# Attention on one core: the mixing of two neighbouring sets in one burst of ten rounds instead of two bursts of five

## Chip, cores, metric

One core of one Trainium2 chip. The time is device microseconds of the whole kernel on that core; lower is better.

## What is computed

The input x is (2, 8, 256, 512): two entries, eight channels, 256 rows (features) of 512 columns. The reference normalises it by groups, runs an attention layer with a residual, normalises again, and runs a 3x3 convolution on a sphere with a residual. The change touches only the attention core of the first layer:

```
qk = jnp.einsum('bceqd,bcekd->bceqk', q, k) / math.sqrt(h)
a = jax.nn.softmax(qk, axis=-1)
o = jnp.einsum('bceqk,bcekd->bceqd', a, v)
...
return _conv(_mcl(o, Wo, bo), o_conv_w, o_conv_b, 0)
```

For every entry and channel (16 in all) there are 8 heads of width 32 over 512 positions. `Wo` is a 256x256 product per channel that follows.

## The kernel before, in words

Three parts run one after the other: `front` (normalisation, projections, convolutions, rotary embedding, to about 410 us), `attend` (attention and the product with `Wo`, to about 979 us) and `blend` (the rest). The change is in `attend`.

One entry and channel is a **unit** (16 units), cut into 32 **steps**: a step is one head and one block of 128 rows or keys. For each step there are

- a row score matmul (L940, 128x512 into one of three PSUM tiles `a_row`) and on VectorE the maximum of each row (L1013). A row matmul waits until the maximum of three steps earlier is done (L938 and L939: `pe.wait_ge(max_done, step - ROWS + 1)`). These maxima serve the next unit.
- a column score matmul (L961, 128x512 into one of two PSUM tiles `a_col`) and on ScalarE its exponential (L1060) into `a_prob`. The column matmul waits for the exponential of two steps earlier (`exp_done, step - 1`).
- the low bf16 part of that exponential (`a_pl`): 26 of 32 steps on GpSimd (L1109), every fifth step on VectorE (L1024), in VectorE's queue right behind the row maximum of that slot.

Four steps are a **set** (eight sets g0 to g7 a unit). `mix_set` (L965 to L985) takes a set's `a_prob` and `a_pl` and does five **rounds**: two that sum the weights (L975) and three that mix the values (L984). A round is four matmuls of 512 columns into four 32-column strips of the array, which run side by side. `a_prob` and `a_pl` are rings of five sets; the first exponential of a set waits for `mixed` of five sets earlier.

After the fourth set of each half unit ScalarE takes the logarithm of the weights (L1065) and inverts it (L1072), and VectorE multiplies (`divide`, L1032, which waits for `inverted`). Once a unit there are four tail parts on TensorE (L998, the product with `Wo`, float32), two copies on ScalarE (L1078), the turning of the maxima (`turn_max` L950, `keep_max` L1048, `load_max` L1052), and the split of the values (`v_high` L1044 on ScalarE, `v_low` L1103 on GpSimd).

The order on each engine is written out by a small scheduler: `pipeline` has one slot for each step of the whole stage; every kind of work is given a slot, and an engine issues slot by slot, in a slot in the order in which the kinds are listed. On TensorE that is: turning, column score, row score, sets, tail parts. The row score of step t of unit n stands in slot 32n + t, the column score in 32n + 42 + t, mixing of set g in 32n + 54 + 4g, tail parts in 32n + 86, 88, 91 and 93, turning in 32n + 35, the half units' logarithm, inverse and `divide` in 32n + 67 and 83, `keep_out` (the copies) in 32n + 90 and 95, `v_high` in 32n + 40. `sets` (L857 and L858) gives the slots of the mixing and is used by TensorE's queue alone. VectorE's low parts stand in slots whose number modulo 32 is 3, 8, 15, 20, 25 and 30 (written as slots of one cycle of 32: 67, 72, 79, 84, 89 and 94).

```
pipeline(units(TURN, turn_max) + steps(EXP, col_scores) + steps(0, row_scores) + sets(MIX, mix_set) + tail_parts(TAIL, tail))
...
pipeline(steps(0, row_max) + units(SPLIT, split_max) + lows(EXP + 1, low_part, False) + quads(KEEP, divide))
```

Of the kernel before, what the change touches and what calls it, by code (L numbers as in the profile page):

```python
# [725 lines left out]
def attend(nc, T, QK, V, Z, mixing, q0, k0, qk0_in):  # L726
# [9 lines left out]
    with ExitStack() as ctx:  # L736
# [3 lines left out]
        STEPS = HEADS * QT  # L740
        UNITS = B * C
        PAIR = B * CHANNELS
        QUAD = P // DH
        SETS = HEADS // QUAD * QT
# [110 lines left out]
            return [(STEPS * n + first + t, lambda n=n, t=t: emit(n, t)) for n in range(UNITS) for t in range(STEPS) if low_on_pool(t) == on_pool]  # L855

        def sets(first, emit):  # L857
            return [(STEPS * n + first + QUAD * g, lambda n=n, g=g: emit(n, g)) for n in range(UNITS) for g in range(SETS)]  # L858

        def quads(first, emit):  # L860
            return [(STEPS * n + first + QUAD * QT * m, lambda n=n, m=m: emit(n, m)) for n in range(UNITS) for m in range(SETS // QT)]
# [70 lines left out]
        def _(pe):  # L932
# [55 lines left out]
            def tail(n, j, part):  # L988
# [10 lines left out]
                if part == PARTS - 1:  # L999
                    last.then_inc(out_full, 1)  # L1000

            pipeline(units(TURN, turn_max) + steps(EXP, col_scores) + steps(0, row_scores) + sets(MIX, mix_set) + tail_parts(TAIL, tail))

        @block.vector
# [669 lines left out]
```

## Time and profile before

| what | value |
|---|---|
| median of 3 runs | 1253.46 us (1249.54 to 1255.03) |
| the profiled execution's own time | 1252.62 us |
| its span | 1250.7 us |
| TensorE busy, whole span | 1075.9 us (86%) |
| VectorE busy | 922.9 us (74%) |
| ScalarE busy | 659.8 us (53%) |
| GpSimd busy | 871.0 us (70%) |
| first and last burst of mixing | 449.8 us and 970.6 us |

Engines in the profile: PE is TensorE (PEld its weight loads), DVE VectorE, ACT ScalarE, POOL GpSimd. Matmuls overlap: the profile gives a 512-column matmul about 0.4 us from start to end, while the next one starts about 0.22 us after it. What counts for TensorE's queue is therefore the distance between starts. In a timeline row the first number is the start, the second the length of what was merged into the row, and the bracket the idle time of the engine ahead of it with what ended it.

### The profile page before, as it was taken

The numbers are of one execution on the slowest core, as the hardware profiler recorded it, in microseconds if no ns is written. First come the engines' busy times: TensorE is split into PE (matmuls) and PEld (weight loads), VectorE is DVE, ScalarE is ACT, GpSimd is POOL, SyncE is SP. The second block draws the span as 40 slices with busy tenths as digits, with TensorE's granted clock in tenths as the row PEclk, the third lists the DMA queues.
The fourth block names the chain that finished last, engine by engine and source line by source line (L and its number), as shares of the span: only waits on it lengthen the run. The fifth ranks groups of instructions, "written<-read, shape, count | busy, mean of one in ns | idle before, by whom it ended". The sixth has DMA issues, their size and how long they took to land. (4 is left out here: it accounts for less than half of the span.)

```text
span 1250.7 us, 25719 instructions
## 1 busy us (share of the span) xinstructions
PE 1075.9 (86%) x10392; PEld 569.9 (46%) x10392; DVE 922.9 (74%) x1225; ACT 659.8 (53%) x1110; POOL 871.0 (70%) x812
## 2 busy tenths in 40 slices
PE   0299999999894699899999999999988599899998
PEld 0177777777673123333333333333333245455553
DVE  3789999999763798788888888888872585544344
ACT  1555555455442066566666676666666233346345
POOL 0467776777583499889998888988899006937900
PEclk9899999999997599999999999999998899899999
DMA  9725243332644545526171726254100599875661
GB/s 306 243 81 161 75 124 114 107 90 74 140 107 103 110 77 133 105 58 114 51 120 35 127 61 111 60 92 75 39 19 17 177 367 295 266 236 156 194 211 54
DMA packets 137757, 158.99 MB, mean 127 GB/s; under 512 B 17852, under 2 KB 85708, under 8 KB 137640
## 3 DMA queue, kind: packets, MB, share of 16 engines
q1 hardware_dynamic: 113448, 119.37, 39.8%
q10 hardware_dynamic: 15648, 28.81, 6.7%
q0 software_dynamic: 8544, 9.18, 2.8%
q8 instruction: 82, 1.34, 0.5%
q14 instruction: 35, 0.29, 0.1%
HBM read 106.48 MB, written 52.89 MB: 127 GB/s over the span
## 5 line engine op out<-in xcount | busy, mean ns | idle before, releaser
L1109 POOL TENSOR_TENSOR a_pl<-a_prob 128x512 bf16<-128x512 f32 x416 | 442.1, 1093 | 38.4 <-ACT a_prob L1060 37.9
L1013 DVE TENSOR_REDUCE a_negmax<-a_row 128x1 f32<-128x512 f32 x512 | 330.0, 705 | 71.2 <-PE a_row L940 70.0
L1060 ACT ACTIVATE a_prob<-a_col 128x512 f32<-128x512 f32 x512 | 288.4, 596 | 151.6 <-PE a_col L961 144.6
L710 POOL TENSOR_TENSOR f_yl<-f_y,f_yh 128x768 bf16<-128x768 f32 x80 | 132.9, 1681 | 95.2 <-ACT f_yh L657 95.2
L657 ACT ACTIVATE f_yh<-f_y 128x768 bf16<-128x768 f32 x80 | 67.4, 844 | 138.4 <-DVE f_y L548 120.3
L450 PE MATMUL f_acc<-f_wh,f_xh 128*32 128x384 bf16 x1280 | 110.1, 332 | 28.1 <-DVE f_wl L538 26.1
L1024 DVE TENSOR_TENSOR a_pl<-a_prob 128x512 bf16<-128x512 f32 x96 | 116.2, 1210 | 20.6 <-ACT a_prob L1060 20.6
L940 PE MATMUL a_row<-k,q 96*128 96x512 bf16 x256 | 106.2, 422 | 22.2 <-PEq L202 15.0
L961 PE MATMUL a_col<-a_q,a_k 98*128 98x512 bf16 x256 | 98.4, 393 | 30.4 <-ACT a_prob L1060 26.4
L961 PE MATMUL a_col<-q,k 98*128 98x512 bf16 x256 | 99.6, 389 | 22.2 <-ACT a_prob L1060 20.7
L714 POOL TENSOR_TENSOR f_straight<-f_straight,f_turned 128x832 f32<-128x832 f32 x40 | 107.2, 2680 | 7.9 <-DVE f_turned L565 7.9
L450 PE MATMUL f_acc<-f_wl,f_xh 128*32 128x384 bf16 x1280 | 109.7, 331 | 0.0
L450 PE MATMUL f_acc<-f_wh,f_xl 128*32 128x384 bf16 x1280 | 109.6, 331 | 0.0
L1373 PE MATMUL b_acc_s<-b_xh,b_mat_h 128*104 128x512 bf16 x256 | 99.4, 388 | 9.8 <-DVE b_xl L1463 8.7
L1375 PE MATMUL b_acc_s<-b_xh,b_mat_l 128*104 128x512 bf16 x256 | 98.5, 385 | 0.0
L1374 PE MATMUL b_acc_s<-b_xl,b_mat_h 128*104 128x512 bf16 x256 | 98.2, 383 | 0.0
L940 PE MATMUL a_row<-a_k,a_q 96*128 96x512 bf16 x256 | 97.7, 382 | 0.3 <-DVE a_negmax L1013 0.3
L1325 POOL DMA_DIRECT2D q<-XP x122 | 60.4, 504 | 33.3 <-ACT b_xn L1559 23.3
L469 PE MATMUL f_acc_qk<-f_band_h,f_yh 128*128 128x208 bf16 x320 | 81.4, 254 | 0.0
L471 PE MATMUL f_acc_qk<-f_band_h,f_yl 128*128 128x208 bf16 x320 | 81.3, 254 | 0.0
L470 PE MATMUL f_acc_qk<-f_band_l,f_yh 128*128 128x208 bf16 x320 | 81.3, 254 | 0.0
L1463 DVE TENSOR_TENSOR b_xl<-b_xn,b_xh 128x513 bf16<-128x513 f32 (+4 forms) x60 | 41.8, 697 | 52.3 <-ACT b_xh L1563 52.2
(156 smaller groups left out, 2185.4 us busy)
## 6 DMA issues: line engine op xcount, KB each, us to landing
X<-b_x ACTq DMA_DIRECT2D x16, 526.0 KB, 8.2
q<-in_x SPq DMA_DIRECT2D x8, 1024.0 KB, 7.7
a_v<-V SPq DMA_DIRECT2D x16, 512.0 KB, 4.3
Z<-a_z ACTq DMA_DIRECT2D x32, 256.0 KB, 2.0
b_z<-Z SPq DMA_DIRECT2D x16, 512.0 KB, 10.9
b_x<-in_x SPq DMA_DIRECT2D x32, 256.0 KB, 10.0
b_res<-X SPq DMA_DIRECT2D x38, 208.0 KB
out<-b_y ACTq DMA_DIRECT2D x38, 208.0 KB
```

The costliest lines, as they stand in the source:

```text
L450: last = nc.tensor.matmul(acc[half][c * KW:(c + 1) * KW, part, 0:PART], xx[g % 2][:, (half * QUAD + c) * FH + f, at], ww[half * QUAD + c][ ...
L710: nc.gpsimd.tensor_tensor(yl[half][n % 2][:], y[half][:], yh[half][n % 2][:], ALU.subtract).then_inc(yl_done, 1)
L714: nc.gpsimd.tensor_tensor(straight[m % 2][:].rearrange("p a m w -> p (a m w)"), straight[m % 2][:].rearrange("p a m w -> p (a m w)"), turn ...
L940: nc.tensor.matmul(row[step % ROWS][:].rearrange("p (t w) -> p t w", t=QT), q[s][0:QK_ROWS, h, qt, m, :], k[s][0:QK_ROWS, h, :, m, :], sta ...
L961: nc.tensor.matmul(col[step % 2][:].rearrange("p (t w) -> p t w", t=QT), k[s][:, h, kt, m, :], q[s][:, h, :, m, :], start=True, stop=True) ...
L1013: nc.vector.reduce_max(negmax[n % PAIR][:, 0, t:t + 1], row[step % ROWS][:], AX.X, negate=True).then_inc(max_done, 1)
L1024: nc.vector.tensor_tensor(pl[p][:, r, :], prob[p][:, r, :], ph[p][:, r, :], ALU.subtract).then_inc(lo_dve, 1)
L1060: nc.scalar.activation(prob[sets_done % RING][:, t % QUAD, :], col[step % 2][:], ACT.Exp).then_inc(exp_done, 1)
L1109: nc.gpsimd.tensor_tensor(pl[p][:, r, :], prob[p][:, r, :], ph[p][:, r, :], ALU.subtract).then_inc(lo_pool, 1)
L1373: nc.tensor.matmul(to, mat_h[:, e, :], xh[s][:, at:at + W], start=first, stop=False)
L1374: nc.tensor.matmul(to, mat_h[:, e, :], xl[s][:, at:at + W], start=False, stop=False)
L1375: last = nc.tensor.matmul(to, mat_l[:, e, :], xh[s][:, at:at + W], start=False, stop=end)
```

## The change

`sets` places set g at `QUAD * (g | 1)` instead of `QUAD * g`: a set with an even number moves by four slots into the slot of its odd neighbour, right ahead of it. The odd sets stay. Mixing stood in slots 54, 58, 62, ... 82 (plus 32n); it stands in 58, 66, 74 and 82, each with two sets, ten rounds one behind the other. In the slot nothing comes between them. No operation, buffer or semaphore is added or taken away.

```diff
         def sets(first, emit):
-            return [(STEPS * n + first + QUAD * g, lambda n=n, g=g: emit(n, g)) for n in range(UNITS) for g in range(SETS)]
+            return [(STEPS * n + first + QUAD * (g | 1), lambda n=n, g=g: emit(n, g)) for n in range(UNITS) for g in range(SETS)]
```

## Rows read from the trace of the kernel before

**Rows 1.** Windows, one unit: stretch, length, busy (instructions) by engine, clock, DMA, GB/s

```profile
701.62:734.83 33.21, 30.19 (x245) 11.47 (x244) 28.04 (x42) 22.23 (x41) 30.01 (x28) 1.00 0.51 91
```

**Rows 2.** Timeline of PE, the bursts' first rounds: start us, length us

```profile
705.98 0.41 PE L975 MATMUL a_weight<-a_prob,a_ones 128*32 128x512 bf16 x4
...
709.31 0.41 PE L975 MATMUL a_weight<-a_prob,a_ones 128*32 128x512 bf16 x4
...
712.64 0.41 PE L975 MATMUL a_weight<-a_prob,a_ones 128*32 128x512 bf16 x4
...
716.67 0.41 PE L975 MATMUL a_weight<-a_prob,a_ones 128*32 128x512 bf16 x4
...
721.58 0.41 PE L975 MATMUL a_weight<-a_prob,a_ones 128*32 128x512 bf16 x4
...
726.39 0.41 PE L975 MATMUL a_weight<-a_prob,a_ones 128*32 128x512 bf16 x4
...
730.31 0.41 PE L975 MATMUL a_weight<-a_prob,a_ones 128*32 128x512 bf16 x4
```

**Rows 3.** The same timeline of PE: what stands before and after bursts

```profile
710.54 0.39 PE L961 MATMUL a_col<-q,k 98*128 98x512 bf16 x1
...
716.36 0.38 PE L940 MATMUL a_row<-k,q 96*128 96x512 bf16 x1
...
722.49 0.39 PE L984 MATMUL a_mix<-a_pl,a_vh 128*32 128x512 bf16 x4
722.81 0.39 PE L961 MATMUL a_col<-q,k 98*128 98x512 bf16 x1
...
723.26 1.03 PE L998 MATMUL a_out<-a_oT,a_wo 128*128 128x256 f32 x4
724.12 0.38 PE L961 MATMUL a_col<-q,k 98*128 98x512 bf16 x1
```

**Rows 4.** Timeline of PE, last unit: one burst right behind another

```profile
968.89 0.40 PE L984 MATMUL a_mix<-a_pl,a_vh 128*32 128x512 bf16 x4
969.10 0.41 PE L975 MATMUL a_weight<-a_prob,a_ones 128*32 128x512 bf16 x4
```

**Rows 5.** Timeline of ACT, same unit as rows 1

```profile
703.78 1.05 ACT L1044 ACTIVATE a_vh<-a_v 128x1024 bf16<-128x1024 f32 x1
...
710.97 2.22 ACT L1060 ACTIVATE a_prob<-a_col 128x512 f32<-128x512 f32 x4 [1.11 <-PE a_col L961]
713.99 0.60 ACT L1065 ACTIVATE a_logs<-a_weight 128x512 f32<-128x512 f32 x1 [0.80 <-PE a_mix L984]
714.49 0.59 ACT L1060 ACTIVATE a_prob<-a_col 128x512 f32<-128x512 f32 x1
714.96 0.63 ACT L1072 ACTIVATE a_inverse<-a_logs 128x512 f32<-128x512 f32 x1
...
728.55 0.68 ACT L1078 ACTIVATE a_z<-a_out,a_bo 128x512 f32<-128x512 f32 x1
```

**Rows 6.** Timeline of DVE, same unit

```profile
715.70 0.69 DVE L1032 TENSOR_TENSOR a_oT<-a_mix,a_inverse 128x512 f32<-128x512 f32 x1 [0.35 <-ACT a_inverse L1072]
...
716.90 1.49 DVE L1024 TENSOR_TENSOR a_pl<-a_prob 128x512 bf16<-128x512 f32 x1
718.32 2.48 DVE L1013 TENSOR_REDUCE a_negmax<-a_row 128x1 f32<-128x512 f32 x4
```

**Rows 7.** Groups by line, same unit: busy us, mean ns, idle before

```profile
L1013 DVE TENSOR_REDUCE a_negmax<-a_row 128x1 f32<-128x512 f32 x32 | 20.5, 681 | 4.8 <-PE a_row L940 4.7
```

**Rows 8.** Timeline of DVE and PE in the first unit

```profile
446.94 3.07 DVE L1013 TENSOR_REDUCE a_negmax<-a_row 128x1 f32<-128x512 f32 x5
447.67 0.39 PE L940 MATMUL a_row<-k,q 96*128 96x512 bf16 x1 [0.56 <-DVE a_negmax L1013]
```

**Rows 9.** Source view of L1024, whole run: shortest, median, longest

```profile
L1024 DVE TENSOR_TENSOR a_pl<-a_prob x96: 673/1223/1527, 445.9 to 967.6; 128x512 bf16<-128x512 f32 x96
```

**Rows 10.** Timeline of POOL, same unit

```profile
707.37 19.36 POOL L1109 TENSOR_TENSOR a_pl<-a_prob 128x512 bf16<-128x512 f32 x18
```

## The prediction

> **What bounds it now.** I read the page's busy shares first, then the waits of the attention stage, then one unit of it in the timelines of all engines. Attention fills 449.8 to 970.6 us with 128 bursts. One unit, from the burst of g4 to the next g4, takes 33.21 us, of which TensorE is busy 30.2, GpSimd 30.0, VectorE 28.0 and ScalarE 22.2 [rows 1]: no engine is full, so the time is set by how they wait for each other. The distances between bursts [rows 1, 2] fall into four pairs, which is how the change groups them:
>
> - A, g5 to g7: 3.33 + 3.33 = 6.66
> - B, g7 to g1 (logarithm, inverse, divide, two tail parts): 4.03 + 4.91 = 8.94
> - C, g1 to g3 (two tail parts, a copy): 4.81 + 3.92 = 8.73
> - D, g3 to g5 (logarithm, inverse, turning, v_high): 8.88, the rest of 33.21
>
> In A the chain runs between TensorE and ScalarE. A burst start is followed 1.23 us later by the next column score [rows 2, 3], 721.58 to 722.81; its exponential starts 0.43 later (710.54 to 710.97); exponentials start 0.54 apart and last 0.60 (four in 2.22 [rows 5]); the column score two steps on follows 0.05 after an exponential's end (my reading of the timelines), its row score 0.22 later, and the burst 0.31 after that (716.36 to 716.67). 1.23 + 0.43 + 0.54 + 0.60 + 0.05 + 0.22 + 0.31 = 3.38, against 3.33 in the trace. ScalarE stands 1.11 us at each burst [rows 5], since only two column tiles are there to feed it. The first half of B carries ScalarE's extra work, and its second half and the first of C are TensorE back to back: both have two tail parts of 0.86 each (723.26 to 724.12 [rows 3]). VectorE waits 4.8 us a unit for row tiles [rows 7]; at 0.60 us a maximum and 1.2 a low part it has work for the rest.
>
> **The change, part by part.**
>
> *Changes of tile shape.* A round is 0.22 us [rows 4] (968.89 to 969.10; five with the way out take 1.23). Into a burst it costs 0.31 where 0.22 is the pace, out of one 0.32 (722.49 to 722.81): about 0.2 a burst more than rounds alone. Joining two saves one such pair, and ten rounds take 1.23 + 1.11 = 2.34 to the next column score. That is 64 x 0.2 = 12.8 us off TensorE's queue; how much is on the path is the question. The Trainium skill (TensorEngine Tiling (Array Packing), Key Properties) says that changing the tiling mode drains the engine; the trace agrees, with 0.1 us each way, and a sum by this rule alone would be 12.8 us faster.
>
> *The chain of A.* Eight steps with one burst: 2.34 + 0.43 + 5 x 0.54 + 0.60 + 0.05 + 0.22 + 0.31 = 6.65, against 6.66. The pair of transitions saved is paid with ScalarE's time: a burst of five hides two exponentials, and so does one of ten. ScalarE stands 2.2 once instead of 1.11 twice. No gain, no loss. VectorE's last maximum before the row score of slot 82 is done in time, as long as it comes to the pair without a backlog.
>
> *B, slots 83 to 90, from the burst of slot 82 at 0.* ScalarE: logarithm at 2.45 (0.1 after the burst ends, as before: 712.64 to 713.99 is 1.35), exponential 2.95, inverse 3.42, done 4.05 [rows 5]. TensorE by itself would start the next burst at 8.60: it waits for the exponentials of 83 and 84 (column scores 85 at 3.60 and 86 at 4.59), then has row 86, tail part (0.86), two pairs of scores (0.88), tail part, two pairs, 0.31. VectorE is what doesn't fit. Row tile 83 is there at 2.56 + 0.41 = 2.97, done 3.57; `divide` waits for the inverse until 4.16 (0.11 after it, as at 715.70 [rows 6]) and takes 0.61; maximum 84 at 4.77; low part 84 at 5.37, as long as the same one before, 1.49 of which 1.41 to the next start [rows 6]; maximum 85 at 6.78. Row score 88 needs 85 done, which TensorE sees 0.73 after its start (446.94 to 447.67 [rows 8]), at 7.51; TensorE alone would issue it at 6.55. Stall 0.96. Before, the burst of g0 stood between rows 86 and 87 and gave VectorE that time; now it is gone. The next burst starts at 9.56: +0.62.
>
> *C, slots 91 to 98.* Same reckoning: row 91 at 2.56, tail parts 2.78 and 4.52, row 94 at 5.60. ScalarE: exponential 95 at 6.34, copy of z at 6.84 (0.57), exponential 96 at 7.41, so that column score 98 comes at 8.06 and TensorE alone would burst at 8.59 (-0.14). VectorE: maximum 94 at 6.01, low part 94 at 6.61, maximum 95 at 8.02; row 98 needs that: 8.75 instead of 8.28, burst 9.06: +0.33.
>
> *D, slots 67 to 74.* Turning after the burst (0.32), logarithm 2.45, exponential, inverse, copy of the maxima, then exponentials 68 to 71 up to 6.36, v_high 6.86 (about 0.95 to the next start, [rows 5]), exponential 72 at 7.81, column score 74 at 8.46, burst 8.99. VectorE's rows are late by some tenths inside but not at the end. +0.11. ScalarE's extra work found some of its room in two idle times before and has one now.
>
> *Sum.* A unit: -0.01 + 0.62 + 0.33 + 0.11 = +1.05, some 34.3 us. Row scores end in slot 511, so B with rows occurs 14 times, C 13, A and D 14: 8.7 + 4.3 + 1.5 - 0.1 = 14.4. In the first unit VectorE is full (five maxima in 3.07 with no gap [rows 8]) and a hole of 2.34 + 0.31 + 0.22 + 0.41 = 3.28 between a row score and the next tile outlasts three waiting maxima (1.8) by 1.5: with a low part often there, about 1 us in all. The last two cycles have no row scores; B there would gain 0.2 to 0.3, and the last sets wait for GpSimd's last low part as before. Together +15.1: 1252.6 + 15.1 = 1267.7 for an execution like the profiled one, which lies 0.8 under the median shown; I take 1268.
>
> *Bounds.* The uncertain term is the low part on VectorE, 0.67 to 1.53 us, median 1.22 [rows 9]. GpSimd runs 18 low parts in a row at 1.075 apart through A and B [rows 10], and which value VectorE gets depends on where in one of them it starts. At 0.67 for 84 and 94, B comes to about 8.75 and C to 8.59: 14 x (-0.2 + 0.1) - 13 x 0.14 = -3, so 1250. At 1.53 everywhere with a backlog left for A and D it is another 0.4 a unit, 1274. I take the same values as before, since both engines start from the same events. The Trainium skill (SBUF — State Buffer, SBUF: two separate sides) says that GpSimd and a VectorE operation with two SBUF inputs exclude each other for a whole instruction; [rows 9] agree, with a span of 0.86 us, somewhat under one GpSimd low part.
>
> *Nothing:* the rings. The first exponential of set G needs set G-5 mixed; even sets are now mixed four slots ahead of that instead of eight, and TensorE has issued them long before the column score. GpSimd's last low part of an odd set is due in the slot where it was, nine slots after its exponential; even sets get four slots more. Weight and mix tiles are overwritten eight slots after the half unit's last burst instead of four. The DMA queues keep their places.
>
> **Rivals.**
>
> *1. VectorE keeps up* (low parts short, or a phase that avoids them). Then B -0.34, C -0.14, D +0.11: 14 x (-0.24) - 13 x 0.14 = -5, 1247.5. For it: VectorE has 4.8 us of idle time a unit [rows 7]. Against: that idle time lies at the bursts, and a longer burst makes more of it.
>
> *2. Faster: TensorE's queue is the bound.* It is busy 30.2 of 33.2 us [rows 1]; if the waits for ScalarE are absorbed, the whole 12.8 comes off: 1240. It decides if ScalarE, fed in one piece, ends its exponentials earlier than TensorE's own work of 28 us a unit needs. Against: in A ScalarE's chain has no slack at all.
>
> *3. Far slower: VectorE or GpSimd becomes the bound of every pair.* Each ten-round burst opens a hole of 3.28 against 2.1 before; if three tiles of cover (1.8) are all there is, it costs about 0.8 more a pair, 58 x 0.8 = 46 us, 1299. Against: VectorE isn't full after the first unit.
>
> *4. The change does nothing*: if an odd set's low parts were always late, its half of the burst would split off. GpSimd is about 3 us ahead of the bursts that I checked; 2%.
>
> **Chances.** Forecast (row queue behind VectorE) 0.62, rival 1 0.20, rival 2 0.10, rival 3 0.06, rival 4 0.02. A measurement can tell some 0.5%, 6.3 us, from nothing. Slower by more: 0.62 (less its short end) + 0.06, 0.66; faster by more: rival 2 and part of rival 1, 0.14; within: 0.20. The range 1245 to 1278 takes in rival 1, both bounds and a little of rival 3.
>
> **What would show it.** Right: between the 10-round bursts distances near 6.65, 9.6, 9.1 and 9.0; row score 88 and 98 waiting for L1013; 64 idle times of ScalarE of about 2.2 us; VectorE waiting more than 4.8 us a unit for rows. Wrong: B at or under 8.9 with no wait of L940 for L1013, or A longer than 6.8 (then I misread the chain), or bursts that wait for GpSimd.

## The result, and the profile after

The changed kernel takes 1289.39 us (median of 4 runs, 1288.08 to 1291.14), the one before 1252.95 (four executions, one more than in the table of before): a ratio of 1.0295, 95% interval 1.0268 to 1.0321. Slower was right; 1268 was not, and 1278, the top of the range, lies 11 us short. The profiled execution took 1290.02, against 1252.62 of the one before: 37.4 us more. All of it is in attention: the last burst starts at 1008.4 instead of 970.6, 37.8 later, and what follows it takes as long as before.

From the page of the changed kernel (PE's clock in the second row, in 40 slices of the span), and the same clock row of the kernel before:

```profile
PE 1107.5 (86%) x10392; PEld 583.5 (45%) x10392; DVE 947.1 (74%) x1225; ACT 657.8 (51%) x1110; POOL 879.5 (68%) x812
PEclk9899999999896598999898898999999799999999
```

```profile
PEclk9899999999997599999999999999998899899999
```

The same instructions, and TensorE is busy 31.6 us longer with them. In the attention stage (about the 15th to the 32nd slice) the changed kernel's clock row has five eights and a seven; the one of before has nines there but for the end, where the last units have less work. The windows view puts numbers on one place, the end of D and the burst that follows (columns: stretch, length, busy us of PE, PEld, DVE, ACT and POOL, PE's clock, DMA share, GB/s):

```profile
719.00:722.80 3.80, 2.54 (x10) 0.46 (x8) 3.80 (x6) 3.54 (x7) 3.38 (x4) 0.98 0.23 63
722.80:729.60 6.80, 6.54 (x45) 1.90 (x46) 4.28 (x5) 1.79 (x4) 5.98 (x5) 0.51 0.44 114
```

From 719.0 to 722.8 TensorE works 2.5 of 3.8 us, in short pieces between waits of at most 0.86 us; ScalarE (3.54) and VectorE (3.80) are full or nearly so. Then the clock is 0.51: its lower level, 1.2 GHz, and the ten-round burst of g4 and g5 falls into it. The timeline of PE, first rounds only:

```profile
715.10 0.41 PE L975 MATMUL a_weight<-a_prob,a_ones 128*32 128x512 bf16 x4
...
724.60 0.62 PE L975 MATMUL a_weight<-a_prob,a_ones 128*32 128x512 bf16 x4
...
726.71 0.64 PE L975 MATMUL a_weight<-a_prob,a_ones 128*32 128x512 bf16 x4
...
733.53 0.41 PE L975 MATMUL a_weight<-a_prob,a_ones 128*32 128x512 bf16 x4
```

A joined set's second half starts 2.11 us after its first (at full clock 1.12), and A is 8.93 us long. The clock falls at the end of D in each of the first 12 units. In six of them the low clock covers the whole long burst and A is 8.8 to 9.1, in the other six a part of it and A is 6.9 to 8.4. But from 873 to 972 us the clock stays up, and there the same kernel shows what the change costs by its waits alone:

```profile
904.18 0.41 PE L975 MATMUL a_weight<-a_prob,a_ones 128*32 128x512 bf16 x4
...
910.84 0.41 PE L975 MATMUL a_weight<-a_prob,a_ones 128*32 128x512 bf16 x4
...
920.49 0.41 PE L975 MATMUL a_weight<-a_prob,a_ones 128*32 128x512 bf16 x4
...
929.59 0.41 PE L975 MATMUL a_weight<-a_prob,a_ones 128*32 128x512 bf16 x4
...
938.65 0.41 PE L975 MATMUL a_weight<-a_prob,a_ones 128*32 128x512 bf16 x4
```

| | before [rows 1, 2] | predicted | after, full clock | after, with a fall |
|---|---|---|---|---|
| A | 6.66 | 6.65 | 6.66 | 6.9 to 9.1 |
| B | 8.94 | 9.56 | 9.65 | 8.9 in 11 units, 9.92 in one |
| C | 8.73 | 9.06 | 9.10 | 9.1 |
| D | 8.88 | 8.99 | 9.06 | 9.2 to 9.6 |
| unit | 33.21 | 34.26 | 34.47 | 36.3 at 724.60 |

The same two units in the windows view (compare [rows 1]):

```profile
904.18:938.65 34.47, 30.32 (x245) 11.94 (x244) 30.50 (x42) 22.08 (x41) 30.50 (x28) 1.00 0.12 39
724.60:760.92 36.32, 32.92 (x246) 12.39 (x245) 29.49 (x42) 22.08 (x41) 30.46 (x28) 0.92 0.44 81
```

Of the step that was forecast, VectorE's queue, the trace shows each link in a unit at full clock. In B `divide`, low part 84 and the maxima after it (timeline of DVE), and row scores 88, in B, and 98, in C, that wait (timeline of PE):

```profile
914.99 0.69 DVE L1032 TENSOR_TENSOR a_oT<-a_mix,a_inverse 128x512 f32<-128x512 f32 x1 [0.48 <-ACT a_inverse L1072]
915.60 0.68 DVE L1013 TENSOR_REDUCE a_negmax<-a_row 128x1 f32<-128x512 f32 x1
916.20 1.58 DVE L1024 TENSOR_TENSOR a_pl<-a_prob 128x512 bf16<-128x512 f32 x1
917.70 3.15 DVE L1013 TENSOR_REDUCE a_negmax<-a_row 128x1 f32<-128x512 f32 x5
```

```profile
918.44 0.39 PE L940 MATMUL a_row<-a_k,a_q 96*128 96x512 bf16 x1 [0.88 <-DVE a_negmax L1013]
...
929.27 0.39 PE L940 MATMUL a_row<-a_k,a_q 96*128 96x512 bf16 x1 [0.32 <-DVE a_negmax L1013]
```

Against the burst at 910.84, `divide` starts at 4.15 (forecast 4.16), the low part at 5.36 (5.37) and takes 1.58 (taken as 1.49).

In 11 of the 12 units with a fall this link of B is missing. Low part 84 comes at the same place there but takes 0.84 us, because it meets GpSimd at another point of its work: GpSimd had caught up in the slow burst and stood waiting for an exponential just before (timelines of DVE and POOL, the B that begins at 733.53):

```profile
738.89 0.84 DVE L1024 TENSOR_TENSOR a_pl<-a_prob 128x512 bf16<-128x512 f32 x1
```

```profile
738.14 5.48 POOL L1109 TENSOR_TENSOR a_pl<-a_prob 128x512 bf16<-128x512 f32 x5 [0.36 <-ACT a_prob L1060]
```

The low part is 0.74 shorter and B 0.72 shorter than at full clock. In the twelfth such unit the low part takes 1.47, and B is 9.92.

**Where the 37.4 us are.** I add them up burst by burst to the last burst, which comes 37.8 later. Over the 12 units with a fall, A is 20.8 us longer in sum than 12 times its 6.66, D 4.8 longer than 12 times 9.06, and B 7.6 shorter than 12 times 9.65: 18.0 us for the clock. The waits are 34.47 - 33.21 = 1.26 a unit, 17.6 over 14 units. The first joined burst starts 2.1 us later than the second burst of before, and the last two units are 3.6 longer. Against that stand 3.4 us that the kernel before loses in one unit: a column score of D waits 2.86 us there for a transfer, D is 10.89 long, the clock falls at 505, and the A behind it takes 8.08 (together 37.9):

```profile
504.79 0.38 PE L961 MATMUL a_col<-a_q,a_k 98*128 98x512 bf16 x1 [2.86 <-DMA a_q<-a_maxrows]
505.01 0.46 PE L940 MATMUL a_row<-a_k,a_q 96*128 96x512 bf16 x1
505.39 0.62 PE L975 MATMUL a_weight<-a_prob,a_ones 128*32 128x512 bf16 x4
```

So the kernel before already held one unit in which a burst at the lower clock cost A 1.4 us.

### The profile page after: what moved, and what is told of

It is laid out like the page before. It is cut to its first block and busy times, and to the rows that moved or that the text cites. A ratio compares the mean times of both kernels' runs of the same rounds, so it can differ in the third digit from the quotient of the medians.

```text
span 1288.1 us, 25719 instructions
## 1 busy us (share of the span) xinstructions
PE 1107.5 (86%) x10392; PEld 583.5 (45%) x10392; DVE 947.1 (74%) x1225; ACT 657.8 (51%) x1110; POOL 879.5 (68%) x812
## 5 line engine op out<-in xcount | busy, mean ns | idle before, releaser
L1109 POOL TENSOR_TENSOR a_pl<-a_prob 128x512 bf16<-128x512 f32 x416 | 456.8, 1126 | 75.4 <-ACT a_prob L1060 75.0
L1013 DVE TENSOR_REDUCE a_negmax<-a_row 128x1 f32<-128x512 f32 x512 | 328.6, 704 | 77.4 <-PE a_row L940 76.9
L1024 DVE TENSOR_TENSOR a_pl<-a_prob 128x512 bf16<-128x512 f32 x96 | 133.3, 1388 | 18.8 <-ACT a_prob L1060 18.7
L940 PE MATMUL a_row<-k,q 96*128 96x512 bf16 x256 | 109.1, 433 | 27.5 <-PEq L202 15.0
L961 PE MATMUL a_col<-q,k 98*128 98x512 bf16 x256 | 102.3, 400 | 19.6 <-ACT a_prob L1060 18.4
L940 PE MATMUL a_row<-a_k,a_q 96*128 96x512 bf16 x256 | 101.0, 395 | 6.9 <-DVE a_negmax L1013 5.7
```

What stands on the lines that cost most here:

```text
L940: nc.tensor.matmul(row[step % ROWS][:].rearrange("p (t w) -> p t w", t=QT), q[s][0:QK_ROWS, h, qt, m, :], k[s][0:QK_ROWS, h, :, m, :], sta ...
L961: nc.tensor.matmul(col[step % 2][:].rearrange("p (t w) -> p t w", t=QT), k[s][:, h, kt, m, :], q[s][:, h, :, m, :], start=True, stop=True) ...
L1013: nc.vector.reduce_max(negmax[n % PAIR][:, 0, t:t + 1], row[step % ROWS][:], AX.X, negate=True).then_inc(max_done, 1)
L1024: nc.vector.tensor_tensor(pl[p][:, r, :], prob[p][:, r, :], ph[p][:, r, :], ALU.subtract).then_inc(lo_dve, 1)
L1109: nc.gpsimd.tensor_tensor(pl[p][:, r, :], prob[p][:, r, :], ph[p][:, r, :], ALU.subtract).then_inc(lo_pool, 1)
```

## Experiments

Theory 1 says this: some 15 us are the row queue (row scores that wait for VectorE) and some 22 the clock, which falls because D no longer has a burst in its middle. Theory 2: the long burst starves the other engines at any clock, and the falls only accompany it. Every ratio is to the kernel before, timed beside it on the same chip.

**TensorE kept at work in D.** The row score matmul of slots 68 to 73 is issued twice.

```diff
-                nc.tensor.matmul(row[step % ROWS][:].rearrange("p (t w) -> p t w", t=QT),
...
-                                 start=True, stop=True).then_inc(row_full, 1)
+                for again in range(2 if 4 <= t <= 9 else 1):
+                    last = nc.tensor.matmul(row[step % ROWS][:].rearrange("p (t w) -> p t w", t=QT),
...
+                                            start=True, stop=True)
+                last.then_inc(row_full, 1)
```

> The changed kernel, with the row score matmul of the six slots 68 to 73 of each cycle issued twice into the same tile (the same result), so that TensorE works through part of its waits in D. Theory 1 (the clock: 15 us of the loss are the waits behind VectorE's queue, as forecast, and some 22 us come from the clock, which falls to its lower level once a unit at the end of D because TensorE stands there): with 1.3 us more work a unit in D the falls vanish or become rare, A goes from 7.9 to 9.0 down to 6.7, and the time from 1289 to 1268 to 1274, although TensorE has 20 us more work. Theory 2 (the falls only accompany the loss; the long burst starves ScalarE and VectorE at any clock): the time stays at 1289 or rises by up to 10.

Measured: 1276.1 us (median), ratio 1.0166 [1.0117, 1.0215]; the profiled execution 1271.29, 18.7 less than that of the changed kernel, though TensorE has 96 matmuls (and 96 weight loads) more. Windows, the same place in the cycle and a whole unit:

```profile
709.40:713.20 3.80, 2.98 (x13) 0.86 (x12) 3.80 (x6) 3.53 (x7) 3.38 (x4) 1.00 0.07 22
714.56:749.03 34.47, 31.14 (x251) 12.60 (x250) 30.48 (x42) 22.08 (x41) 30.49 (x28) 1.00 0.49 85
```

No fall in 14 units, each with A 6.66, B 9.66, C 9.11, D 9.07: 34.5. Theory 2 would have kept the time. This run sets the price of the clock, some 18 us of the profiled executions, and that of the waits. The profiled execution is the fastest of its four, with the highest granted clock (0.965; the others 0.955 to 0.963). By the ratios, 1.0295 and 1.0166, the doubling brings back 16 us, and the median lies 2 us above the expected range.

**Control: the same doubling in the kernel before.**

> Control: the kernel before with the same doubled row scores. The clock is at its higher level there anyway, so the doubling can only cost: 1252 to 1260 (0 to 0.4 us a unit). If it is faster by more than 4 us, then the doubling helps in some other way, and the run of the changed kernel with it says less about the clock.

Measured: 1262.1 us, 1.0072 [1.0047, 1.0096]; a unit is 33.87 instead of 33.21. The doubling does not help by itself: here it costs 0.66 a unit, two thirds more than I had allowed for, and the median lies 2 us above the expected range.

```profile
706.99:740.86 33.87, 31.42 (x252) 12.17 (x252) 29.08 (x42) 22.29 (x42) 30.18 (x28) 1.00 0.49 87
```

**Three pairs of four: g4 keeps its slot.** Shown here and in the next run is only the piece of the line in `sets`, against the changed kernel.

```diff
-QUAD * (g | 1)
+QUAD * (g if g == 4 else g | 1)
```

> The change for three of the four pairs: g4 stays in its own slot, the others are joined. D keeps a burst in its middle. Theory 1: no fall of the clock between D and A; B 9.6 and C 9.1 as in the changed kernel at full clock, D and A together about 0.1 longer than before: 34.2 us a unit, 1267 us in all. Theory 2: the loss is shared by the pairs, so three quarters of it stay: about 1280.

Measured: 1269.2 us, 1.0110 [1.0062, 1.0159], profiled 1264.3. B 9.59, C 9.11, D and A together 15.53 (before 15.54), and from 470 to 950 us no fall:

```profile
693.90:728.10 34.20, 30.04 (x252) 11.78 (x248) 29.06 (x42) 22.09 (x40) 30.41 (x28) 1.00 0.81 122
```

34.2 was expected and 1267 in all. The three joined pairs cost what the row queue costs, and with a burst in the middle of D the clock stays up.

**The pair g4, g5 alone.**

```diff
-QUAD * (g | 1)
+QUAD * (g | 1 if g == 4 else g)
```

> The change for the pair g4, g5 alone. Theory 1: D has no burst in its middle and TensorE stands there; the clock falls in most units, A is 8 or more instead of 6.7, B and C keep their 8.9 and 8.7: 1265 to 1278, though at full clock this kernel should be within 3 us of the one before. Theory 2: a quarter of the loss, about 1262, with the clock high.

Measured: 1271.2 us, 1.0131 [1.0090, 1.0172]. The clock falls in 12 of the first 14 units; a whole one and the place where it falls:

```profile
737.78:771.85 34.07, 31.64 (x245) 11.89 (x244) 29.45 (x42) 22.20 (x41) 30.17 (x28) 0.95 0.34 72
741.00:745.00 4.00, 2.84 (x8) 0.63 (x8) 4.00 (x7) 3.75 (x8) 3.58 (x5) 0.80 0.02 4
745.00:749.00 4.00, 4.00 (x44) 1.32 (x44) 3.65 (x4) 1.15 (x3) 4.00 (x3) 0.77 0.10 32
```

D, from the burst of g3 to the joined one, is about 8.38 with a fall and 7.95 and 7.99 in the two units that have none; the next distance is about 4.75 instead of 4.44. So a fall costs 0.7 us here and 1.5 on average in the whole change (18.0 over 12), where in six units the whole long burst lies in it. One pair of four brings nearly half of the whole loss (16.7 of 36.4 us by the medians), and of its 0.86 us a unit 0.72 is the clock.

**VectorE's low parts out of the way.** In the changed kernel they go to other steps.

```diff
+        ON_DVE = (3, 7, 15, 23, 27, 31)
...
-            return t % EVERY != EVERY - 1
+            return t not in ON_DVE
...
-            return DVE_LOWS * n + QUAD * (g + 1) // EVERY
+            return DVE_LOWS * n + sum(t < QUAD * (g + 1) for t in ON_DVE)
```

> The changed kernel, with VectorE's six low parts of a unit moved out of the way: to the steps 3, 7, 15, 23, 27 and 31 (slots 78, 82, 90, 98, 70, 74), four of them right at a burst, where VectorE has nothing else. The row scores of slots 88 and 98 then don't wait for VectorE: B 8.6 and C 8.6 instead of 9.6 and 9.1 at full clock. Theory 1: 1.4 us a unit, some 20 us, come back: 1268 to 1272, less if the clock still falls and more if it stops. If the low parts only lengthen there by GpSimd's port, B stays above 9.2 and the time above 1280.

Measured with step 3: 1276.2 us, 1.0154 [1.0112, 1.0195], above the expected 1268 to 1272. B 8.62 and C 8.61, as expected, so the row queue's term is shown. But A is 7.95 at full clock: I had put one low part where it does the same harm, ahead of the maximum that row score 82 waits for.

```profile
681.21 1.57 DVE L1024 TENSOR_TENSOR a_pl<-a_prob 128x512 bf16<-128x512 f32 x1
```

```profile
683.44 0.39 PE L940 MATMUL a_row<-k,q 96*128 96x512 bf16 x1 [1.10 <-DVE a_negmax L1013]
```

With step 4, the low part behind that maximum:

> The run before the last without the doubled row scores: the changed kernel with VectorE's low parts at 4, 7, 15, 23, 27 and 31 alone. Row queue repaired, clock not: B and C 8.6, and D and A disturbed by falls in part of the units, at about 1.5 to 2 us each: 1255 to 1270. If the clock stays high here, then the falls need the row waits of B and C as well, and it equals the run with both.

Measured: 1258.1 us, 1.0037 [1.0011, 1.0063]. A unit at full clock has A 6.66, B 8.61, C 8.60, D 9.07:

```profile
707.46:740.40 32.94, 29.70 (x245) 11.96 (x245) 28.05 (x42) 22.08 (x41) 30.48 (x28) 1.00 0.44 89
```

The clock falls in three of the first 14 units (at 471, 574 and 905 us) instead of 12, although D is as long as in the changed kernel. So the emptier end of D is what brings the 12 falls (doubling its row scores, or leaving g4 in it, took them all away), but it does not always bring one. In the changed kernel too, the same stretch has the same load with a fall behind it and without (two windows of one run, at the same distance behind the burst of g3; the clock falls at the end of the first and not behind the second):

```profile
681.62:685.42 3.80, 2.54 (x10) 0.46 (x8) 3.80 (x6) 3.55 (x7) 3.38 (x4) 0.96 0.02 4
899.00:902.80 3.80, 2.54 (x10) 0.46 (x8) 3.80 (x6) 3.53 (x7) 3.38 (x4) 1.00 0.03 6
```

The DMA queues are nearly idle in both (2 and 3%), so their traffic isn't what decides between the two. Nor is an emptier D the only way to a fall: the one of the kernel before at 505 stands behind its wait for a transfer.

**Both repairs at once.**

> The changed kernel with both repairs: the row score matmul issued twice in slots 68 to 73 (the clock), and VectorE's low parts at steps 4, 7, 15, 23, 27 and 31 (slots 79, 82, 90, 98, 70, 74). The run with step 3 showed A at 7.95 at full clock, since the low part of slot 78 stood before the maximum that row score 82 waits for; at slot 79 it stands behind it. If both terms of the loss are what theory 1 says, nothing of it is left: A 6.66, B 8.62, C 8.61, D 9.07, 32.96 a unit against 33.21 before, no fall of the clock: 1247 to 1253. If a third term is there, the time stays above 1260.

```profile
706.08:739.00 32.92, 30.60 (x251) 12.64 (x250) 28.00 (x42) 22.07 (x41) 30.46 (x28) 1.00 0.53 89
492.79:506.13 13.34, 8.34 (x67) 3.08 (x66) 8.90 (x13) 6.98 (x13) 11.10 (x10) 0.88 0.86 200
```

Measured: 1260.6 us, 1.0064 [1.0039, 1.0089]; the profiled execution 1254.9. The unit is 32.92, as reckoned and less than before's 33.21; the total is not. One D, at 492.79, takes 13.34: a column score waits 4.34 us there for the transfer of the maxima, in a stretch in which the DMA queues move 200 GB/s, and the clock falls in it. Before has such a wait too, of 2.86 us. With that and the first unit the gain of 0.29 a unit is gone in the profiled run. The median misses the expected 1247 to 1253 and lies just over the 1260 that I had set as the sign of a third term, and it is no better than that of the low parts alone (1258.1). Why it lies 6 us above the profiled execution stays open; an execution of 1261.98 had a granted clock of 0.966, above the 0.964 of the profiled one, so the clock doesn't explain that one.

**The other direction: bursts cut in two.** In the kernel before, the two rounds of weights stand two slots ahead of the three of mixing.

```diff
-            pipeline(units(TURN, turn_max) + steps(EXP, col_scores) + steps(0, row_scores) + sets(MIX, mix_set) + tail_parts(TAIL, tail))
+            pipeline(units(TURN, turn_max) + steps(EXP, col_scores) + steps(0, row_scores) + sets(MIX - 2, weigh_set) + sets(MIX, mix_set) + tail_parts(TAIL, tail))
```

> The kernel before, with the change's direction turned round: each burst of five rounds is cut in two, the two rounds of weights two slots ahead of the three of mixing. By the chain of A ScalarE stands at a burst because it has two column tiles to live on (1.1 us); bursts of two and three rounds would cover that, at the price of 0.2 us more of tile changes a set. D and B's first half, where ScalarE carries extra work, should lose most of their two holes: D 8.9 to some 8.0, A 6.67 to 6.7, B 8.9, C 8.5: 32.1 a unit, 1235 to 1242. If the changes of tile shape decide instead (TensorE the bound), it is slower by up to 13 us: 1265.

Measured: 1248.5 us, 0.9972 [0.9951, 0.9993]: 0.3% faster, about a third of what I expected. VectorE is now 30.27 us busy in a unit of 33.07; its low part of slot 72 runs into GpSimd's split of the values (2.13 us) and takes 2.66 (timelines of DVE and POOL, then the unit):

```profile
702.56 2.66 DVE L1028 TENSOR_TENSOR a_pl<-a_prob 128x512 bf16<-128x512 f32 x1
```

```profile
702.54 2.13 POOL L1107 TENSOR_TENSOR a_vl<-a_v,a_vh 128x1024 bf16<-128x1024 f32 x1 [0.58 <-ACT a_vh L1048]
```

```profile
701.47:734.54 33.07, 31.24 (x245) 10.63 (x244) 30.27 (x42) 22.30 (x42) 30.23 (x28) 1.00 0.51 89
```

**The same, that low part two slots earlier** (steps 4, 9, 14, 19, 24, 27), and the move alone in the kernel before.

> The cut bursts (weights two slots ahead of mixing) with one of VectorE's low parts moved from step 29 to 27. In the run with cut bursts VectorE was busy 30.3 of 33.1 us a unit and its low part of slot 72 took 2.66 us, because it met GpSimd's v_low of 2.1 us; row scores waited for it. Two slots earlier it should take 1.0 to 1.5: 1.2 us a unit less on a queue that is now nearly full: unit 32.0 to 32.6, 1233 to 1243. If TensorE's queue (31.2 us) is what holds it, nothing changes: 1248.

> Control: the kernel before with that low part moved alone. Its low part of slot 72 takes 0.67 us there and VectorE has 4.8 us to spare: no gain, 1251 to 1256; D may grow by some tenths.

Measured: 1242.8 us, 0.9923 [0.9892, 0.9955], the fastest of all; alone 1252.3 us, 1.0000 [0.9978, 1.0023]. In the cut kernel it takes 0.68 us now, less than the 1.0 to 1.5 expected, and a unit 32.26, which shows that VectorE's long low part was on the path:

```profile
731.07 0.68 DVE L1028 TENSOR_TENSOR a_pl<-a_prob 128x512 bf16<-128x512 f32 x1
```

```profile
698.91:731.17 32.26, 31.07 (x245) 10.64 (x245) 27.97 (x42) 22.33 (x42) 30.19 (x27) 1.00 0.51 91
```

**The pair g0, g1 alone**, where TensorE was full, with low parts at 4, 7, 15, 19, 24 and 29.

> The change for the pair g0, g1 alone, the one between the tail parts where TensorE was back to back, with VectorE's low parts of steps 9 and 14 moved to 7 and 15 so that they don't stand before row score 88. One pair of tile changes comes off a queue that is full there, and the row score doesn't wait: B and C together 17.3 instead of 17.7 us, D 8.9 and A 6.7 as before, no fall of the clock: 32.9 a unit, 1246 to 1250. If the joined pair costs ScalarE what it saves TensorE, 1253.

Measured: 1251.7 us, 0.9990 [0.9968, 1.0011]: no difference that can be told. The unit at 661.89 is 33.06 against 33.21 (32.9 was expected); B and C together 17.5 instead of the 17.3 expected. Before they were 17.7.

## Why the prediction was right and wrong

- **The pace of A, right.** "No gain, no loss": 6.66 before and after. Joining two bursts takes one pair of tile changes away (the second half follows 1.12 us after the first), and ScalarE's longer stand takes it back.
- **B and C, right at full clock.** 9.65 and 9.10, forecast 9.56 and 9.06, by the links named: `divide`, low part 84, row score 88; low part 94, row score 98. In the changed kernel itself only two of 14 units show B so; the run with doubled row scores shows it in all 14. Moving the low parts makes both 8.6, the value that the reckoning gave TensorE by itself (8.60 and 8.59).
- **D, right in its length, wrong in what was read from it.** 9.06 for 8.99. The failed step is the sum: it multiplies lengths at full clock by the number of units (for A, "-0.01" in all 14) and has no term for the clock, which it put at nothing without a reason. [rows 1] said 1.00, and the prediction took that for given, although the kernel before had the unit at 505 us in which a fall had cost A 1.4. In D the change takes a burst out of a stretch in which TensorE waits for ScalarE; it then works 2.5 of 3.8 us, the clock falls to 1.2 GHz, and the longest burst of the cycle pays for it. 12 falls, 18 us; doubling the row scores of the stretch, or leaving g4 in it, brings the 18 us or most of them back.
- **The sum otherwise.** 1.26 us a unit for 1.05. With the clock kept up the changed kernel's profiled execution took 1271.3, for 1267.7 forecast.
- **The signs named.** Row scores 88 and 98 wait for L1013 as named. The other two signs were off even at full clock: ScalarE stands 2.22 us in A, but 1.90 and 2.40 before the logarithms and 1.70 and 1.63 in the two other places; and VectorE waits for rows 3.5 us a unit, not more than 4.8. Its six low parts take 9.2 us there instead of 7.2 and fill that time; the one of slot 72 went from 0.67 to 2.05, beside GpSimd's split of the values (2.14).
- **Rivals.** The first (VectorE keeps up) falls with B and C. The second (TensorE's queue is the bound) falls with A; in B and C without the row waits, where TensorE is back to back, the change is worth 0.1 to 0.3 us each. The third comes nearest in size, by another mechanism: every pair bound by VectorE isn't there, since A keeps its 6.66. None of the four, and neither end of the range, had the clock in it. The Trainium skill (TensorE: Matmul & The Clock Gate, What's actually happening) says that the clock is set by how busy TensorE has been recently, and calls the lower state idle. The runs agree with the first: 2.98 us of work instead of 2.54 in the same 3.80, and the falls are gone. But the engine wasn't idle: it was at work in short pieces, and no single wait in D ahead of the fall near 722.8 was longer than 0.86 us.

What stays open: why the full-clock units of the changed kernel, and most of the run with low parts moved, go through the same end of D without a fall; and why the run with both repairs is not faster than the kernel before. The low clock's part in the executions that were not profiled is known from their mean granted clock alone.

## What to carry to other kernels

When a change takes dense work out of one stretch and piles it up in another, read for each stretch what TensorE is left with, not only how long it gets: an emptier stretch can halve the clock for the dense one behind it, and here that cost as much as the waits did (18.0 and 17.6 us). Look in the trace of before for a unit that already has such a fall: it gives the price. With two column tiles and three row tiles, cutting bursts (and moving the one queue entry that then collides) gained 0.8% where joining lost 3%. I take from it that long bursts want deeper buffers at their consumers; no run changed the buffers.

## What the runs showed of the hardware that was not expected

- The clock fell to 1.2 GHz behind a stretch in which TensorE worked 2.54 of 3.80 us and never stood for more than 0.86 (at 719.0 in the changed kernel); and the same stretch at 899.0, also with 2.54 of 3.80, brought no fall.
- A VectorE operation with two SBUF inputs (the low part) that took 0.68 us where GpSimd stood takes 2.66 us beside a GpSimd operation of 2.13. The Trainium skill (SBUF — State Buffer, SBUF: two separate sides) describes this as a lock for the whole instruction, held by whichever of the two starts first; the trace agrees: GpSimd's operation starts at 702.54, VectorE's at 702.56, and it ends 0.55 after the other.
- A fall gives a little back: behind it, in 11 of 12 units, low part 84 took 0.84 us instead of 1.58 and B 8.9 instead of 9.65, because GpSimd had caught up in the slow burst. Where the low part took 1.47 behind a fall, B was 9.92. The rows show this; no run was made for it.
